# Turning the recurrence's outputs to rows of tokens with the identity less the mean over a head

## The reference

```python
def step(s, rkvw):
    r_t, k_t, v_t, w_t = rkvw
    a = k_t[..., :, None] * v_t[..., None, :]
    out = jnp.einsum('bhi,bhij->bhj', r_t, u * a + s)
    s = a + w_t[..., :, None] * s
    return (s, out)
_, out = jax.lax.scan(step, s0, rkvw)
out = jnp.moveaxis(out, 0, 1).reshape(b, l, e)
og = out.reshape(b, l, h, s_)                 # h = 32 heads of s_ = 8
m = og.mean(-1, keepdims=True)
va = ((og - m) ** 2).mean(-1, keepdims=True)
og = ((og - m) / jnp.sqrt(va + 1e-05)).reshape(b, l, e) * gn_w + gn_b
x1 = x + og * g @ Wo.T
```

## Time and profile before

| | |
|---|---|
| median of 3 runs | 1938.76 us (1938.2 to 1943.43) |
| profiled execution | 1946.16 us, of which the span is 1944.4 us |
| TensorE matmul | 1855.2 us busy, 14320 instructions |
| VectorE | 1113.0 us busy, 2104 instructions |
| ScalarE | 1042.5 us busy, 1945 instructions |
| GpSimd | 998.8 us busy, 1140 instructions |
| the recurrence | about 389 to 617 us of the span |

### The profile page before, as it was taken

The page is one execution under the profiler, slowest core; times in us unless marked ns, Lnnn a source line. Parts: engine busy times, 40 slices in busy tenths (PEclk is TensorE's granted clock), DMA queues, the critical chain, the costliest instruction groups (busy, mean ns, idle before and its releaser), DMA issues.

```text
span 1944.4 us, 37701 instructions
## 1 busy us (share of the span) xinstructions
PE 1855.2 (95%) x14320; PEld 1507.0 (78%) x14320; DVE 1113.0 (57%) x2104; ACT 1042.5 (54%) x1945; POOL 998.8 (51%) x1140
## 2 busy tenths in 40 slices
PE   7999999989986999999999999999999998999899
PEld 5777789534454788888888888888888887967788
DVE  3656756389989555444444544544444545746654
ACT  4556543434344655665655656656665654345532
POOL 6777731376654544554554544544454535257620
PEclk9999999999998999999999999999999999999999
DMA  6000010000001223223223322322322310010000
GB/s 240 2 2 2 2 58 1 1 1 1 1 1 49 82 66 104 82 86 98 90 83 96 96 82 85 106 82 82 109 83 82 110 44 1 22 44 2 1 12 33
DMA packets 61842, 108.01 MB, mean 56 GB/s; under 512 B 7009, under 2 KB 42337, under 8 KB 60257
## 3 DMA queue, kind: packets, MB, share of 16 engines
q1 hardware_dynamic: 60784, 103.38, 16.9%
q10 hardware_dynamic: 880, 2.22, 0.3%
HBM read 103.47 MB, written 2.10 MB: 54 GB/s over the span
## 4 chain that ended last, share of the span: by engine, by line
PE 84%; DVE 7%; issue 3%; POOL 3%; ACT 2%; DMA 0%; DVEq 0%; SPq 0%; ACTq 0%; POOLq 0%
PE banks L864 18%; PE banks L935 9%; PE banks L892 9%; PE banks L471 7%; PE banks L629 7%; PE banks L646 6%; PE banks L924 6%; PE banks L905 3%; PE banks L480 3%; PE banks L528 2%; PE banks L553 2%; PE banks L539 2%; PE banks L510 2%; PE banks L465 2%; PE banks L913 1%
## 5 line engine op out<-in xcount | busy, mean ns | idle before, releaser
L1984 POOL TENSOR_TENSOR w_lo<-w2ring,w_hi 128x512 fp32r<-128x512 f32 x128 | 179.9, 1406 | 245.1 <-ACT w_hi L1130 245.1
L1806 DVE TENSOR_REDUCE nmax<-banks 128x4 f32<-128x260 f32 x128 | 54.2, 423 | 308.7 <-PE banks L905 308.7
L2067 POOL TENSOR_TENSOR wo_lo<-wo_ring,wo_hi 128x256 fp32r<-128x256 f32 x128 | 93.2, 737 | 250.6 <-ACT wo_hi L1338 250.4
L1794 DVE TENSOR_TENSOR v<-banks,dbv 128x512 f32<-128x512 f32 x128 | 88.5, 691 | 158.8 <-PE banks L892 158.7
L1338 ACT ACTIVATE wo_hi<-wo_ring 128x256 fp32r<-128x256 f32 x128 | 53.2, 417 | 190.3 <-PE banks L935 189.4
L935 PE MATMUL banks<-wo_hi,c_hi 128*128 128x256 f32 x512 | 149.0, 291 | 4.4 <-DVE c_lo L1799 4.4
L935 PE MATMUL banks<-wo_lo,c_hi 128*128 128x256 f32 x512 | 146.2, 286 | 0.0
L935 PE MATMUL banks<-wo_hi,c_lo 128*128 128x256 f32 x512 | 146.1, 285 | 0.0
L1325 ACT ACTIVATE k<-banks,cols 128x512 f32<-128x512 f32 x128 | 88.1, 689 | 80.4 <-PE banks L864 80.4
L924 PE MATMUL banks<-PT,v 128*128 128x128 f32 x1024 | 124.7, 275 | 1.0 <-issue 0.8
L924 PEld LDWEIGHTS banks<-PT,v 128*128 128x128 f32 x1024 | 119.7, 192 | 1.6 <-issue 1.2
(11 more groups left out here) (235 smaller groups left out, 5436.3 us busy)
## 6 DMA issues: line engine op xcount, KB each, us to landing
w2ring<-in_w SPq DMA_DIRECT2D x128, 384.0 KB, 3.2
b2ring<-in_b SPq DMA_DIRECT2D x128, 128.0 KB, 3.9
wo_ring<-in_wo SPq DMA_DIRECT2D x128, 128.0 KB, 3.4
mlp_w<-in_mlp SPq DMA_DIRECT2D x6, 1024.0 KB, 7.4
wl<-in_wres SPq DMA_DIRECT2D x1, 2688.0 KB, 8.8
X<-in_x_in SPq DMA_DIRECT2D x4, 512.0 KB, 11.3
wb<-in_wres SPq DMA_DIRECT2D x2, 1024.0 KB, 11.1
ctxT<-in_ctx_in SPq DMA_DIRECT2D x4, 512.0 KB, 18.4
```

Source lines behind the costliest of these rows:

```text
L1794: V.tensor_tensor(v2[i], held(("v2", v, i)).rearrange("p (s d) -> p s d", s=HV), dbv, ALU.add).then_inc(S["l2_v"], 1)
L1984: G.tensor_tensor(w2_lo[:, n % 2, :], w2ring[:, n % HR, 0:2 * KT * P], w2_hi[:, n % 2, :].bitcast(f32), ALU.subtract).then_inc(S["l2_wlo"], 1)
L2067: G.tensor_tensor(wo_lo[:, n % 2, :], wo_ring[:, n % WR, :], wo_hi[:, n % 2, :].bitcast(f32), ALU.subtract).then_inc(S["l2_wolo"], 1)
```

## The change

The products with the identity become products with a table `center`, of 128 + 2 x 256 columns, made on the host and loaded by SyncE behind the L1 weights into the place of bias rows that are no longer used. Its first 128 columns are the identity less 1/8 within each head. The other two parts, of 256 columns each, do the same for the two halves of oS, with the reordering of the channels in them: so each product with oS now has all 256 columns as its output, plain, where it had 128 strided ones. What arrives in PSUM has its mean over each head taken out. VectorE's sum and centring are gone, and its multiplication waits for l1_cent. ScalarE copies each half from PSUM to gn, at j = 4 and 5, behind the state column of that piece; its squares stand at j = 5 and 6 in place of 5 and 7. After the last chunk ScalarE does both copies and the first square ahead of `fronts(EARLY)`. The tile gn_sum is gone, and the tiles behind it move by 128 words.

```diff
+        center = at("center", held_to[0] - len(ROWS) * D, P + 2 * D)
+        center_f, center_s = center[:, 0:P], view(center[:, P:], "p (q n) -> p q n", q=2)
...
-        gn_sum = view(keep("gn_sum", 2 * 64), "p (s g) -> p s g", s=2)
...
 def tokens_first(c):
+                    if c == 0:
+                        pe.wait_ge(s_center, 16)
...
-                                mm(out[:, k * P:(k + 1) * P], rku[c % 2][:, k, tok], ident, start=(i + k == 0), stop=False,
+                                mm(out[:, k * P:(k + 1) * P], rku[c % 2][:, k, tok], center_f, start=(i + k == 0), stop=False,
                                    skip_group_check=True)
                             for q in range(2):
-                                last = mm(out.rearrange("p (x q j) -> p q j x", q=2, j=4)[:, q], oS[:, q, tok], ident,
+                                last = mm(out, oS[:, q, tok], center_s[:, q],
                                           start=False, stop=(i + q == 2), skip_group_check=True)
...
 def after(c, j):
-                    if j in (5, 7):
-                        h = (j - 5) // 2
+                    if j in (5, 6):
+                        h = j - 5
                         act.wait_ge(S["l1_cent"], 2 * c + h + 1)
                         if h:
                             act.wait_ge(S["l1_var"], 2 * c + h)
                         A(norm_tiles(c)[0], gn[:, h, :], ACT.Square).then_inc(S["l1_sq"], 1)
+                    if j in (4, 5):
+                        h = j - 4
+                        act.wait_ge(S["l1_og"], 2 * c + h + 1)
+                        if c:
+                            act.wait_ge(S["l1_gn_tp"], KT * c)
+                        A(gn[:, h, :], held(("og", c, h)), ACT.Copy).then_inc(S["l1_cent"], 1)
...
                     normed(EARLY)
+                    after(last, 4)
                     after(last, 5)
                     fronts(EARLY)
-                    act.wait_ge(S["l1_og"], 2 * CHUNKS)
                     for n in range(2):
                         weights_hi(n)
                         value_weights_hi(n)
-                    after(last, 7)
+                    after(last, 6)
                     after(last, 9)
...
 def group_norm(c, h, piece):
-                    if piece == 0:
-                        dve.wait_ge(S["l1_og"], 2 * c + h + 1)
-                        if c:
-                            dve.wait_ge(S["l1_gn_tp"], KT * c)
-                        og = held(("og", c, h)).rearrange("p (g j) -> p g j", j=S8)
-                        settle(V.tensor_reduce(gn_sum[:, h, :], og, AX, ALU.add))
-                        V.scalar_tensor_tensor(xg, gn_sum[:, h, :].unsqueeze(2).to_broadcast([P, 64, S8]), -1.0 / S8,
-                                               og, ALU.mult, ALU.add).then_inc(S["l1_cent"], 1)
...
+                        dve.wait_ge(S["l1_cent"], 2 * c + h + 1)
                         V.tensor_tensor(xg, xg, root[:, h, :].unsqueeze(2).to_broadcast([P, 64, S8]), ALU.mult).then_inc(S["l1_gn"], 1)
...
-                    if j in (4, 5, 6, 8, 10, 11):
-                        group_norm(c, *{4: (0, 0), 5: (1, 0), 6: (0, 1), 8: (1, 1), 10: (0, 2), 11: (1, 2)}[j])
+                    if j in (6, 8, 10, 11):
+                        group_norm(c, *{6: (0, 1), 8: (1, 1), 10: (0, 2), 11: (1, 2)}[j])
...
                 load_weights(sp, s_wl1, wl1, "L1_m1", "L1_W")
+                sp.dma_start(center, t_center).then_inc(s_center, 16)
...
+def centering():
+
+    p, f = np.arange(P), np.arange(D)
+    parts = [np.eye(P) - (p[:, None] // S8 == p[None, :] // S8) / S8]
+    for q in range(2):
+        same = p[:, None] % 32 == f[None, :] // S8
+        parts.append(same * ((4 * q + p[:, None] // 32 == f[None, :] % S8) - 1.0 / S8))
+    return np.concatenate(parts, axis=1).astype(np.float32)
```

More of the change, by code:

```diff
@@ L136, with build @@
 NWRES = _at
-def build(nc, t_x, t_ctx, t_state, t_ltor, t_cross, t_bmask, t_cols, t_rows, t_consts, t_wres, t_mlp,
+def build(nc, t_x, t_ctx, t_state, t_ltor, t_cross, t_bmask, t_cols, t_rows, t_consts, t_center, t_wres, t_mlp,
           t_w2, t_b2, t_wo2, t_out):
@@ L345, in build @@
             sem, ("vectors_in", "w_qkv_in", "w_self_in", "w_cross_in", "w_l1_in", "w_l3_in", "preset", "masks_in", "rows_in", "state_in"))
-        s_ident, s_rows0, s_sel = sem("ident_in"), sem("first_rows_in"), sem("select_in")
+        s_ident, s_rows0, s_sel, s_center = sem("ident_in"), sem("first_rows_in"), sem("select_in"), sem("center_in")
         s_x = [sem(f"x_in{c}") for c in range(CHUNKS)]
@@ L1778, in rwkv @@
                     split(CHUNKS * L2A)
-                    after(last, 4)
-                    after(last, 5)
                     after(last, 6)
@@ L2309 @@
         "bmask": g("mask_BxS2_bf1").view(np.uint8).reshape(CHUNKS, NT, 2, SEQ).transpose(2, 0, 1, 3).reshape(2, CHUNKS * NT * SEQ),
-        "cols": cols, "rows": rows, "consts": shape_constants(), "wres": wres, "mlp": mlp,
+        "cols": cols, "rows": rows, "consts": shape_constants(), "center": centering(), "wres": wres, "mlp": mlp,
         "w2": np.concatenate(w2), "b2": np.concatenate(b2), "wo2": np.stack(wo2),
```

## The result

The changed kernel takes 1944.5 us (median of 20 runs, 1941.56 to 1949.18), the kernel before 1940.3 us (20 runs, 1937.72 to 1943.43): +4.2 us, a ratio of 1.0023 with a 95% interval of 1.0016 to 1.0030. The forecast was +3.5 us, from 1938.76 to 1942.3 us; 1.5 us of the 2.2 us between 1942.3 and 1944.5 lie in the median of before, which came out at 1940.3 this time. The time is not 0.3% longer, so by the bound set ahead it counts as no change, but the interval leaves 1 out: the change costs a little.

The account below looks back on a forecast made before the run. In the recurrence VectorE and TensorE are both nearly full, with TensorE's token products ahead of VectorE's step 5. Boundary terms 0.7 + 1.7 + 1.1 = +3.5 us take 1938.76 to 1942.3 us; range 1936.5 to 1947.5.

Parts of the forecast that it names:

- The price of the columns: TensorE's token products with oS over 256 columns: 16 passes a chunk grow by 0.105 us, +1.7 us a chunk.
- The upper bound: Wide token products: at most 0.216 us more per pass, a full second pass at 1.2 GHz, 3.4 us a chunk.
- A: Chunk boundary at 450 us: products +1.68, second half's sum and centring gone -1.31, net +0.37 us.
- B: Chunk boundary at 506 us: same rows as at 450 us, net +0.37 us.
- C: Chunk boundary at 566 us, chunk 3: VectorE's saving falls into idle time, longer products arrive whole, +1.7 us.
- rival 4: Second PSUM bank waits for ScalarE beyond 0.9 us of slack: a tenth or so each; chance 0.02.
- let it catch up by 468 us: After the first two boundaries TensorE, 1.3 us late against VectorE, recovers through its waits of 0.6 and 0.7 us.
- rival 3: TensorE becomes the recurrence's bound: +6.1, 1944.9 us; with one boundary's token products at lower clock 1950.1; chance 0.17.
- About 4 us idle before step 7 at C: Sign in the profile after: VectorE about 4 us idle before step 7 at the 566 us boundary; before, 2.57 us.
- D: After chunk 3, up to the next stage's first matmul: ScalarE's copies ahead of hT, +1.1 us; bounds +0.8 to +1.7.
- (1): Columns are cheap: wide products cost nothing beyond the weight load, -1.6, 1937.1 us; chance 0.09.
- (2): VectorE's work counts: 2.7 us saved at each of three boundaries inside the loop, -7.0, 1931.8 us; chance 0.08.

Follow-up runs that it names:

- wide_only: Kernel before with only the new table and its wide products, VectorE still summing and centring, no ScalarE copies: 1946.99 us, 1.0026.
- narrow: Changed kernel with the oS products back at 128 strided columns and the identity, output not the reference's: 1937.71 us, 0.9981.
- filled: Changed kernel repeating mix and v products ahead of two TensorE waits in chunks 1 and 2, results unchanged: 1942.88 us, 1.0011.
- before_v_first: Kernel before with the token products moved behind the v products of step 5 on TensorE: 1940.81 us, 0.9996.
- after_end_order: Changed kernel; after the last chunk, second-half token products go behind the transposes and ScalarE's second copy behind hT: 1943.14 us, 1.0013.
- after_v_first: Changed kernel with the token products moved behind the v products of step 5 on TensorE: 1940.53 us, 0.9994.

## Why the prediction was right, point by point

**What was right.** *The price of the columns.* 0.105 us more a pass from the earlier trace rows, forecast +1.68 us a boundary: wide_only measured 1.67, 1.68 and 1.68. It was the term with most against it: from the figures for 128 and 512 columns in the Trainium skill, TensorE: Matmul & The Clock Gate, section Back-to-back issue gap, follows an estimate of 0.27 us a chunk. The trace doesn't agree with that for these f32 products, and the row of this kernel was the better guide. The upper bound was argued badly: at the lower clock a pass of 256 columns would take some 0.43 us (an estimate, twice 0.216), 0.32 more than before's 0.111 and not 0.216. It was not needed, for the token products ran at clock 1.00 at A in both kernels.

*What of VectorE's saving counts.* The forecast gave the first half's pair 0 and the second's 1.31 at A and B, both 0 at C. narrow measured 1.30, 1.31 and 0.0. VectorE's idle time before step 5 was forecast at 3.9 us and is 3.88.

*A, B and C.* Forecast +0.37, +0.37 and +1.7; measured +0.35, +0.35 and +1.67.

*ScalarE and the banks (rival 4).* The copies take 0.58 us (median 578 ns of 8), the second of A runs from 456.07 to 456.64, and the wait put down to it is 0.36 us of one weight load (456.98), which in before is 0.35 us and has another cause. At C the second copy ends at 575.88, while the output products (L482) run from 575.52 to 578.89 and come to their second half at about 577.2.

*The table's load.* Issued behind the L1 weights and landed 9.3 us later, 186 us ahead of its first use at 446.89, at no cost:

```profile
251.66 0.44 SPq L2187 DMA_DIRECT2D center<-in_center  x1
```

**What was missed.** The sum ends each boundary with "let it catch up by 468 us" and has no term behind that. TensorE did catch up, already by 463.86 us. What was put at nothing is the lower clock on the head sums and projections that come next: it added 1.47 and 1.64 us to them, 1.2 us of air took up the most of it, and 0.34 us behind A and 0.54 behind B remained, 0.9 in all. The prediction had read the 0.79 of the earlier trace rows and used it for rival 3 alone, as something that would meet the token products; it met the projections instead. In before the stretch of the earlier trace rows began 6.5 us earlier, counted from the first scan (71.7 us against 78.6, of which 0.4 is the lag at A), and cost nothing, which made it look harmless. It also hid how much air there is: the waits of 0.6 and 0.7 us are those of a chunk in which the lower clock had used up one more, and at B before has 0.62, 1.38 and 0.66 us. filled shows the cause: with the waits filled the clock stays and the 0.9 us are gone.

**A row put in the wrong place.** "About 4 us idle before step 7 at C" did not come: it is 2.58 us there, as before. The shift at C is as forecast, but the idle time stands ahead of steps 5 and 6, where the two pairs and the longer products were; the forecast had added it to the one wait that it had read.

**A term that was too large.** D was put at +1.1 us and is +0.87. The timeline of after:

```profile
625.53 1.04 PE L467 MATMUL banks<-consts,xn 128*128 128x128 f32 x8
625.73 0.60 ACT L1221 ACTIVATE gn<-banks 128x512 f32<-128x512 f32 x1
626.22 1.44 ACT L1021 ACTIVATE hT<-banks,cols 128x512 f32<-128x512 f32 x2
...
631.33 1.22 PE L868 MATMUL banks<-ctx_hi,w_hi 128*128 128x512 f32 x2 [4.76 <-POOL w_lo L1985]
```

From the start of the second copy to that of hT it is 0.49 us, since neighbouring instructions of ScalarE overlap, where the forecast added 0.6 and a gap; hT starts right when the transposes allow, and so the lower of the two bounds, that of the transposes, was the one to take (transposes 0.85 us late behind 3, 15, hT 0.87). narrow says the same of ScalarE's chain: without the wide products it costs 0.73, not 1.0. The errors have opposite signs: 0.9 missed, 0.2 to 0.3 too much in D and the rounding. That they partly cancel is luck; the sum of +3.5 is 0.6 to 0.7 short of the 4.1 to 4.2 measured.

**The rivals.** (1) and (2) fall, with wide_only and narrow. (4), the bank, cost nothing. (3), TensorE becomes the bound of the recurrence, was half right. Its mechanism as stated, a lag that exceeds the air in the chunk, did not occur, and A and B didn't cost 1.68 each; but its "second half", the granted clock, is what the missing 0.9 us are.

**What stays open.** Why the clock falls behind some waits and not behind others was not settled. The same waits as after's, 0.99 and 0.65 us, stand in chunk 1 of narrow, and longer ones, 1.36 to 1.38 and 0.63 to 0.66 us, in chunk 2 of before and of wide_only and in chunk 1 of before_v_first, and the clock stays up in all four. So that the change pays 0.9 us is what its two profiles and that of after_end_order show, not a law of the kernel. In before_v_first the 2.3 us lost from chunk 3 on were only read, not tested, nor were the smaller steps of 0.2 to 0.8 us that wide_only, narrow and filled take between 3, 6 and 3, 15. And the sizes at C and D rest on the scans of single profiles, though these repeat to 0.2 us.

## What to carry to other kernels

Where two engines walk in step and both look nearly full, work taken from one is worth what stands behind the other's last delivery, not its duration: here 10.9 us off VectorE were worth 2.6, and 6.7 us onto TensorE cost 5.0 in the loop, because each boundary runs TensorE, ScalarE, VectorE in a fixed order. So read the waits right ahead of and right behind the moved work, boundary by boundary, and expect a reordering to move the wait to the next instruction in the queue (xm in after_v_first, w_hi in after_end_order). Where two chains run side by side, as at D, the costs of the parts don't add up: the later chain counts. And when full work stands right behind a wait of TensorE, look at the granted clock on that work, in more than one profile: a stretch at the lower clock costs what it takes beyond the air behind it, here 0 to 0.5 us for 3.4 us of it.

## What the runs showed of the hardware

At A the clock fell to the lower level for 3.4 us behind a TensorE wait of 0.99 us and within one of 0.65 us, and at B behind waits of 0.98 and 0.64 us, in both profiles of the changed kernel. Such waits don't bring it every time: in narrow, chunk 1, 0.99 and 0.65 us were followed by clock 1.00, and in before, chunk 2, 1.38 and 0.66 us as well. With repeated products in these waits the clock stayed at 1.00 through both stretches, and the end of chunk 2 came 0.89 us earlier: more work took less time. The medians (2.25 us above the one of before beside it for filled, 4.2 us for after) point the same way, but their intervals overlap, so the scans and the granted clock carry this, not the times.

At clock 1.00 an f32 product costs 0.215 us a pass over 256 columns and 0.11 over 128, whether these are plain or strided in PSUM: narrow's strided groups of four passes (L705) take 0.45 us from start to start, as the plain ones (L702) do. With weight loads of 0.19 us beside every pass, none of the added columns was hidden.
